# A two-layer cross-attention and mixture-of-experts kernel: order of the work in its first stage

## The reference

```
x = x + L0_xattn(ctx, layernorm(x))      # 4 heads of 64; keys and values from the context and from x itself
x = x + L0_ffn(layernorm(x))             # 8 experts, the best 2 per token, relu, 1024 wide
x = x + L1_xattn(layernorm(x), ctx)      # 16 heads of 16; keys and values from the context alone
x = x + L1_ffn(layernorm(x))             # 8 experts, the best 2 per token, gated, 512 wide
```

## Time and profile before

| | |
|---|---|
| median of 3 runs | 1573.96 us (1572.23 to 1576.97) |
| the profiled execution | 1573.92 us |
| its span | 1572.2 us |
| TensorE busy | 1430.4 us (91%) |
| DVE busy | 1036.2 us (66%) |
| ACT busy | 829.4 us (53%) |
| POOL busy | 685.5 us (44%) |

### The profile page before, as it was taken

One profiled execution on the slowest core, in us unless ns is written; L12 is line 12 of the kernel. 1 busy time (PEld: TensorE's weight loads), 2 busy tenths in 40 slices (PEclk: granted clock), 3 DMA queues, 4 the chain that ended last, 5 costly groups with the idle time before them and its releaser, 6 DMA issues. The chain is left out here.

```text
span 1572.2 us, 35956 instructions
## 1 busy us (share of the span) xinstructions
PE 1430.4 (91%) x12426; PEld 1048.7 (67%) x12426; DVE 1036.2 (66%) x1991; ACT 829.4 (53%) x1513; POOL 685.5 (44%) x525
## 2 busy tenths in 40 slices
PE   8799999999986699999999978999978499999996
PEld 2433333333355589989899966777758389999885
DVE  5678888888768645555555427888958755455443
ACT  2678888887743245556555524667744032222221
POOL 2522212211110254555545425777752246666554
PEclk6899999999975699999999996999995599999998
DMA  5332333232238365556577433000016274334553
GB/s 166 111 108 82 102 115 132 82 115 74 81 105 299 110 181 132 145 141 161 130 200 192 103 71 107 23 6 28 29 30 240 86 226 68 62 66 68 109 136 49
DMA packets 114589, 175.77 MB, mean 112 GB/s; under 512 B 18992, under 2 KB 76644, under 8 KB 114148
## 3 DMA queue, kind: packets, MB, share of 16 engines
q1 hardware_dynamic: 84375, 132.93, 25.6%
q0 software_dynamic: 27264, 37.82, 13.7%
q10 hardware_dynamic: 2791, 2.84, 0.6%
HBM read 106.34 MB, written 67.23 MB: 110 GB/s over the span
## 5 line engine op out<-in xcount | busy, mean ns | idle before, releaser
L1601 PE MATMUL e_ph<-e_zTt,weights_a 128*128 128x256 f16 x3072 | 350.4, 275 | 2.0 <-DVE e_zTt L1695 2.0
L1601 PEld LDWEIGHTS e_ph<-e_zTt,weights_a 128*128 x3072 | 302.6, 99 | 39.4 <-issue 2.5
L1655 ACT ACTIVATE e_h<-e_ph,e_b 128x256 f32<-128x256 f32 (+1 forms) x312 | 123.6, 453 | 185.9 <-PE e_ph L1601 185.6
L1551 POOL DMA_INDIRECT token_rows<-e_ysb,slot_token x71 | 128.4, 1808 | 172.2 <-DVE e_ysb L1734 158.0
L1615 PE MATMUL e_pyt<-weights_b,e_hh 128*128 x1136 | 192.7, 273 | 1.2 <-DVE e_ysb L1734 1.1
L1541 POOL DMA_INDIRECT gathered<-token_parts,slot_token x138 | 141.6, 1026 | 54.4 <-issue 46.7
L1717 DVE TENSOR_TENSOR e_hl<-e_h,e_hh 128x512 f16<-128x512 f32 x142 | 94.8, 690 | 103.5 <-ACT e_hh L1666 103.5
L680 PE MATMUL middle_banks<-probs,v 128*64 128x512 f32 (+1 forms) x576 | 152.9, 613 | 8.7 <-ACT raw_o L811 7.9
L1551 POOL DMA_INDIRECT out_dram<-e_ysb,slot_token x71 | 113.2, 1594 | 106.0 <-DVE e_ysb L1737 75.1
L935 DVE TENSOR_TENSOR acc<-acc,probs 128x1024 f32<-128x1024 f32 (+1 forms) x112 | 138.6, 1238 | 27.4 <-ACT probs L804 24.8
L1615 PE MATMUL e_pyt<-weights_b,e_hl 128*128 x568 | 154.8, 273 | 0.0
(11 more groups left out here) (274 smaller groups left out, 2805.6 us busy)
## 6 DMA issues: line engine op xcount, KB each, us to landing
weight_parts<-w_split SPq DMA_DIRECT2D x32, 512.0 KB, 3.4
weights_a<-weight_parts SPq DMA_DIRECT2D x16, 1024.0 KB, 7.4
x_sb<-weight_parts SPq DMA_DIRECT2D x14, 1024.0 KB, 6.9
x_sb<-in_u SPq DMA_DIRECT2D x24, 512.0 KB, 4.9
weight_parts<-x_sb SPq DMA_DIRECT2D x24, 512.0 KB, 3.4
w_raw<-in_w1T SPq DMA_DIRECT2D x16, 512.0 KB, 4.4
w_raw<-in_w2T SPq DMA_DIRECT2D x16, 512.0 KB, 4.8
weights_b<-weight_parts SPq DMA_DIRECT2D x8, 1024.0 KB, 9.5
```

Source lines behind the costliest of these rows:

```text
L1551: pool.indirect_dma_start(g.rows[layer], at, ysb[:, s, c, :], None, compute_op=ALU.add).then_inc(sto[s], 16)
L1601: last = pe.matmul(out[:, f, :], weights_up(i, e, wp, k, per[i] * q + f), zTs[:, s, 2 * zp + k, 0:cols[i] * P], start=(n == 0), stop=(n == 5))
L1655: last = act.activation(parted(hidden(h32, n), i)[:, f, :], parted(ph[:, bank_of(i, q)], i)[:, f, :], ACT.Relu, bias=b1[:, bass.ds(e, 1), ...
```

## The change

- ACT issues 11 loads instead of 14: gain and shift of the context norm come as one array put together on the host (`ln_x`), and those of the token norm likewise on SP (`ln_l`). Layer 2's value weights go ahead of its mask, its key weights and the small rows. Each group has a semaphore of its own.
- SP loads batch 0 of the tokens right behind the context, then the projection weights, batch 1, the small rows, batches 2 and 3. At the stage's end it waits only for the small rows.
- TensorE makes layer 2's values right behind the first turn (four idle products between), in the upper half of `kv`'s banks; then comes the turn of `zc`, layer 2's keys, and last the context's keys and values. Layer 2's mask is put on the turned context (DVE) and no longer on the keys, and ACT spreads the keys with a factor per partition that holds the scale.
- Row statistics, summary and root in this stage are those of batch 0 alone. Batch 1's are taken in the attention's head (two tiles in each of four steps), batches 2 and 3 in the slots of batch 0 (one tile a slot), with roots on POOL after tile 5 and after batch 1's roots.
- The context's keys leave the stage raw (`kraw`), with the sums of their squares (`ssc`). Root, norm, halves and the turning of the halves are done in the attention's head, the turning in the upper banks ahead of the first `turn_parts`.

The diff, cut to its core:

```
 # first stage, sync
-sp.wait_ge(ld_w, 32)
-for i in range(B): (load token rows of batch i)
+rows_in(0)
 (load wqkv, wo0)
+rows_in(1)
+sp.dma_start(g.glbl[:], a["ln_l"]).then_inc(ld_small, 16)
 (load bo)
+for i in range(2, B):
+    rows_in(i)
+sp.wait_ge(ld_small, 32)
-sp.wait_ge(ld_next, 16 * 5)
-for arrived in g.x_in:
-    sp.wait_ge(arrived, 16)
 # first stage, scalar: order behind the products
+act.wait_ge(v1_mm, 1)
+act.wait_ge(made, 3)
+own_v = kv[:, 2:4, :].rearrange("p b (h o d) -> p b h o d", o=2, d=HD1)
+for b in range(2):
+    for o in range(2):
+        act.copy(g.v1[:, 2 * b:2 * b + 2, o:H1:2, o * HD1:(o + 1) * HD1].rearrange("p b h d -> p (b h) d"),
+                 own_v[:, b, :, o, :]).then_inc(v1_ev, 1)
+act.wait_ge(k1_mm, 1)
+act.wait_ge(odd_known, 1)
+for hg in range(2):
+    for o in range(2):
+        act.activation(g.k1[:, :, hg, o, :], tr[:, hg, 0:B * M].rearrange("p (b m) -> p b m", b=B), ACT.Copy,
+                       scale=odd_head[:, o:o + 1]).then_inc(k1_ev, 1)
 act.wait_ge(ld_next, 16 * 2)
 (high halves of wqkv, wo)
 act.wait_ge(kv_done, 1)
 act.activation(sq[:], kv[:, :, 0:D], ACT.Square).then_inc(sq_done, 1)
+act.copy(g.kraw[:], kv[:, :, 0:D]).then_inc(sq_done, 1)
 act.copy(g.vctx[:], kv[:, :, D:2 * D]).then_inc(sq_done, 1)
 # first stage, tensor
 turn(ctx, 0)
-keep_going(14)
+keep_going(4)
+pe.wait_ge(ld_v1, 32)
+pe.wait_ge(ev, 2)
+(layer 2's values into kv[:, 2 + b // 2, ...])
 pe.wait_ge(v_step, 13)
 turn(zc, 2)
-keep_going(4)
+pe.wait_ge(ld_k1, 32)
+pe.wait_ge(mask_step, 5)
+(layer 2's keys from the masked context into tr[:, hg, ...])
 pe.wait_ge(ev, 4)
 pe.wait_ge(ld_w, 32)
 for b in range(B):
+    if b == 2:
+        pe.wait_ge(v1_ev, 4)
     (keys and values of the context)
-(layer 2's values and keys, turning of the key halves)
 # attention, tensor, scalar, gpsimd, vector
+        if t < 2:
+            pe.wait_ge(kt_ev, 2)                  # in turn_parts
-pipeline([(turn_z, 0, 2), (project, 1, 2), (turn_parts, 4, 0),
+pipeline([(turn_z, 0, 2), (project, 1, 2), (lambda l: l == 0 and turn_context(), CONTEXT_AT, 0), (turn_parts, 4, 0),
+context_high()                                    # scalar, behind gain_and_shift(1)
+          (lambda l: l == 0 and context_out(), CONTEXT_AT, 0), (parts_out, 4, 0),
+pool.tensor_tensor(rnc[:], g.ssc[:], g.neghalf[0:M, 0:B * H0], ALU.pow).then_inc(kr_done, 1)
+for t in range(TB // 2):
+    root(t, t % 2)
+pool.wait_ge(kt_ev, 2)
+        if t == TB - 3:
+            roots(pool, g, 2, TB, 2 * TB, g.first_steps, g.first_roots)
+    if b == 1:
+        roots(pool, g, 3, 2 * TB, T, g.first_steps, g.first_roots)
+    if t in (TB, 2 * TB):
+        dve.wait_ge(g.first_roots, t // TB + 1)   # in center
+context_norm()                                    # vector, behind ln_low(1)
+context_low()
+          (second_rows, 1, 0),
+        if b == 0:
+            later_rows(j)
+def second_rows(l):
+    if l >= TB // 2:
+        return
+    dve.wait_ge(g.x_in[1], 16)
+    for t in (TB + 2 * l, TB + 2 * l + 1):
+        dve.bn_stats(g.stats[:, t, :], g.x[:, t, :]).then_inc(x_step, 1)
+    if l == TB // 2 - 1:
+        dve.wait_ge(x_step, TB)
+        summarise(dve, g, 2, TB, 2 * TB, True, g.first_steps)
+def later_rows(j):
+    if j < 2 * TB:
+        t = 2 * TB + j
+        dve.wait_ge(g.x_in[t // TB], 16)
+        dve.bn_stats(g.stats[:, t, :], g.x[:, t, :]).then_inc(x_step, 1)
+    elif j == 2 * TB:
+        dve.wait_ge(x_step, 3 * TB)
+        summarise(dve, g, 3, 2 * TB, T, True, g.first_steps)
```

More of the change, by code:

```diff
@@ L123, in attention0_inputs @@
         lnT = m.sb("lnT_c", [P, 2, B, M])
-        gx = m.sb("gx", [P, 2])
-        bx = m.sb("bx", [P, 2])
+        gbx = m.sb("gbx", [P, 4])
+        gx, bx = gbx[:, 0:2], gbx[:, 2:4]
+        ctxT = m.sb("ctxT", [P, 2, 2, B, M])
+        wk1 = m.sb("wk1", [P, 2, D])
+        wv1 = m.sb("wv1", [P, 2, D])
+        own = m.sb("own", [P, 8])
+        own2 = m.sb("own2", [P, 8])
+        odd_head = m.sb("odd", [P, 2])
         wqkv = m.sb("wqkv", [P, 2, 3 * D])
@@ L307, in _ @@
-            dve.wait_ge(v_step, 20)
+            dve.wait_ge(ld_q, 16 * 3)
+            dve.scalar_tensor_tensor(g.gain[:], gq[:], SCALE0, gk[:], ALU.mult, ALU.mult).then_inc(g_step, 1)
+            dve.wait_ge(g_step, 1)
+            dve.tensor_reduce(gabs[:], g.gain[:], AX.X, ALU.max, apply_absolute_value=True).then_inc(g_step, 1)
+            dve.wait_ge(g_step, 2)
+            dve.tensor_scalar(g.shift[:, B:B + 1], gabs[:], -float(HD0), None, ALU.mult).then_inc(g_step, 1)
+            dve.tensor_scalar(g.shift[0:M, 0:B], mask[:], 1.0, -MASKED, ALU.subtract, ALU.mult).then_inc(g_step, 1)
@@ L398, in summarise, with roots @@
     dve.tensor_scalar(ve, tmp[:, 0, :], grow / D, eps, ALU.mult, ALU.add).then_inc(steps, 1)
[L401 to L404 removed]
+def roots(pool, g, run, t0, t1, steps, rooted):
+    pool.wait_ge(steps, 7 * run)
+    pool.tensor_tensor(g.rstd[:, t0:t1], g.stat_ve[:, t0:t1], g.neghalf[:, t0:t1], ALU.pow).then_inc(rooted, 1)
 def attention0(nc, g, a):
@@ L507, in attention0 @@
         LAG = 4
+        CONTEXT_AT = 3
         def pipeline(stages):
@@ L725, in between, with turn_context @@
                     project(tile)
+            def turn_context():
+                pe.wait_ge(kh_done, 1)
+                pe.wait_ge(kl_done, 1)
+                for n in range(2):
+                    for h in range(2 * B):
+                        last = pe.transpose(hi[:].bitcast(F16)[:, n, h * MP:h * MP + M],
+                                            khl[:, n, 2 * h:2 * h + 2, :].rearrange("p o d -> p (o d)"), g.ident16[0:M, 0:M])
+                last.then_inc(kt_done, 1)
             turn_z(0)
@@ L827, in output_high, with context_high, context_out @@
                 act.copy(o16[:, 0, u % 2], oT[:, u % 2]).then_inc(o_hi, 1)
+            def context_high():
+                act.wait_ge(kn_done, 1)
+                act.copy(khl[:, 0], kn[:]).then_inc(kh_done, 1)
+            def context_out():
+                act.wait_ge(kt_done, 1)
+                for n in range(2):
+                    act.copy(g.kctx[:, n, :, 0:M],
+                             hi[:].bitcast(F16)[:, n, 0:2 * B * MP].rearrange("p (h m) -> p h m", m=MP)[:, :, 0:M]
+                             ).then_inc(kt_ev, 1)
             gain_and_shift(0)
             gain_and_shift(1)
+            context_high()
             squares(0)
             squares(1)
-            pipeline([(gain_and_shift, 0, 2), (squares, 1, 2), (high, 3, 0), (parts_out, 4, 0),
+            pipeline([(gain_and_shift, 0, 2), (squares, 1, 2), (high, 3, 0),
+                      (lambda l: l == 0 and context_out(), CONTEXT_AT, 0), (parts_out, 4, 0),
                       (lambda l: l in pieces_head and weight_high(pieces_head[l]), 1, 0),
@@ L1134, in _ @@
         def _(pool):
-            roots(pool, g, 3 + 2 * layer, LAST, T)
+            roots(pool, g, 2 + 2 * layer, LAST, T, g.stat_steps, g.stat_roots)
             pool.iota(rev[:], pattern=[[-1, E]], base=E, channel_multiplier=0,
```

238 lines of the change are left out of this document (94 added, 144 removed).

## The result

The changed kernel takes 1575.81 us (median of 20 runs, 1572.64 to 1579.13) against 1571.70 for the kernel before on the same chip (20 runs, 1565.78 to 1576.97): ratio 1.0029, 95% interval 1.002 to 1.0038, so 3.1 to 6.0 us slower. I had forecast 15 us faster; the rival that was nearest is B, the low clock. The kernel before has two kinds of execution: of 80 taken beside the experiments, 41 have a mean granted clock of 0.922 or more and a median of 1567.8 us, and 39, like the profiled one (0.917), have 0.921 or less and a median of 1573.8 us, while 19 of the changed kernel's 20 lie at 0.913 to 0.919; the ratios here are to the mixture. The profiled execution of the changed kernel has a span of 1572.4 us.

A forecast was written before the change was run, and what follows sets the result against it. The first stage was taken to be bound by a TensorE chain of products at granted clock 0.50. 1573.92 - 19.2 (first stage) + 3.2 (head) + 0.8 (batch 0) = 1558.7 us; 8-in-10 range 1554.7 to 1578.

The forecast's parts named there:

- B: Rival, first stage: low clock returns, products take 30.4 us, attention starts at 41.9 (-4.3); 1573.6 us, no change; chance 0.46 to A, 0.38 to B.
- Start of the products: First stage: TensorE starts layer 2's value products at 7.9 us, behind ACT's 11 loads and two copies.
- the late end: First stage: products start at 10.1 us if the value weights' load again takes 7.6 us.
- the early end: First stage: products start at 7.9 us, with one megabyte of token rows around the weight loads instead of four.
- B's first reason: First stage: the clock is low because the products start late; the other reason was that its first rise fails.
- A: The forecast itself: high clock holds in the first stage, products take 15.4 us; 1558.7 us; chance 0.46.
- My argument against A from float32: First stage: the products are float32 throughout, which was held to speak against the high clock holding.
- Tail: First stage's end: ACT's squares and two copies, 3 x 1.02 = 3.1 us, plus 0.54 before the first `center`.
- Head: Attention's tiles 0 to 7: key work hidden, DVE's added statistics and summary on the path; +3.2 us, between 0 and 4.8.
- Batch 0: Attention's batch 0: 7.3 us more DVE work, mostly in idle time, and tile 16's `center` waiting for a root; +0.8 us.
- Rival C: Batch 0: DVE's added work ends up on the path, 7.3 us in place of 0.8; slower, 1580.1 us; chance 0.16.
- The sum: Whole kernel: first stage -19.2, head +3.2, batch 0 +0.8 against 1573.92 us, giving 1558.7 us.

The follow-up runs named there:

- e6_order_alone: The changed kernel with only ACT's loads reordered: value weights first, context's own weights behind layer 2's key weights; 1557.0 us, ratio 0.9903 to the kernel before.
- e10_sp_held: The changed kernel with SP waiting for the value weights before issuing batch 0's rows and all behind them; 1558.4 us, ratio 0.9942 to the kernel before.
- e8_all_rows: The changed kernel with all four batches' row statistics, summaries and roots in the first stage; 1572.3 us, ratio 1.0008 to the kernel before.
- e3_rows_back: The changed kernel with batch 1's row statistics, summary and root moved back into the first stage; 1571.7 us, ratio 1.0011 to the kernel before.

## Why the prediction was wrong, point by point

- **Start of the products: the step that failed.** ACT's side was right (last issue ends at 7.44, forecast 7.1; copies done at 8.2, forecast 7.9). I then took 7.9 for the start and kept 10.1, the old 7.6 us for the value weights, as the other end. They took 7.4 and 8.1, and TensorE was released at 11.21. So even the late end was too early: it went by the first of the two loads, and the trace before had the second at 8.5 us (shown with the result), which from 3.06 gives 11.6. My reason for the early end, one megabyte of rows now where four stood before, counted only batch 0 and left out the projection weights and batch 1, which SP issues before or beside them. `e6_order_alone`, with the value weights issued ahead of those loads, and `e10_sp_held`, with those loads held back, put the start at 8.72 and 8.38. The Trainium skill, "DMA: Bandwidth & Descriptors", section "Issuing engines are not separate DMA queues", which I quoted and outweighed, says that SP's and ACT's transfers interleave on the same engines; the trace agrees (8.1 us for 64 KB beside SP's loads, 3.8 without).
- **Clock.** Rival B's mechanism, for B's first reason, the late start. Its price was near: 30.4 us of products forecast, 30.2 measured; it came from 11.2 and not 7.9, which with a tail 0.4 shorter makes -1.6 of its -4.3. A's price was near too: 15.4 forecast, 16.3 in `e6_order_alone`, which lands at 1557.0 where A stood at 1558.7. My argument against A from float32 falls. The same products are busy 16.20 of 16.28 us at 1.00 in `e6_order_alone`. The Trainium skill, "TensorE: Matmul & The Clock Gate", section "Why this matters for your kernels", says that keeping TensorE continuously busy gets it to the high clock. The trace of the change disagrees again: busy 30.19 of 30.20 us at 0.50.
- **Tail.** 3 x 1.02 + 0.54 = 3.6 forecast; 41.4 to 44.6, 3.2, measured: right to 0.4.
- **Head.** +3.2 forecast, +4.26 measured. DVE's statistics are 2.8 of it (3.1 against `e8_all_rows`), within 2.5 to 3.55; the 1.5 of the second fall of the clock (1.1 against `e8_all_rows`) was not in the sum. That the key work would be hidden there is neither shown nor refuted.
- **Batch 0.** +0.8 forecast, +1.0 measured; without the statistics (`e8_all_rows`) +0.5. `center` of tile 16 waits for POOL, but DVE idles only 0.44 there. Rival C did not happen.
- **The sum.** -1.6 + 4.3 + 1.0 = +3.7 by the marks of the two profiles, 3.1 to 6.0 by the times. The two do not measure the same: the profile before is of the kind at the lower mean clock, the times are to both kinds.

## What to carry to other kernels

Where a chain of TensorE bounds a stage, read the granted clock and the last idle stretch ahead of it before its order: here that level was worth 13.5 us at the first `center` (44.60 against 31.14), the new order with the clock held 2.8 at tile 16's turn (174.04 against 176.82). For the first operand of a chain that is moved forward, add up all bytes that any queue has issued before it lands. Work taken out of a stage into a full engine's queue is paid there, so part each mark of the path and look at all parts. Before a median is used as a yardstick, list the mean granted clock of every execution behind it: here the kernel before had two kinds, 6 us apart, and one profile shows only one of them.

## What the runs showed of the hardware that was not expected

- The same float32 products ran at 0.50 for 30.2 us in the change and at 1.00 for 16.3 us in `e6_order_alone`, busy nearly without a break in both (30.19 of 30.20 us, 16.20 of 16.28). In `e10_sp_held` they began at 0.53 us each and went on at 0.30, so the clock can rise while they run. What decides is not shown.
- The granted clock reads 1.00 from the start of these profiles, though six warm-up matmuls at 2.51 take 0.46 us each, and 0.23 each later; in `e10_sp_held` it reads 1.00 from 8.38 to 10.40 beside products of 0.53 us. Ahead of the first fall that a profile's rows show, go by the length of the matmuls.
- The length of one idle stretch does not tell alone whether the clock falls: 1.72 us ahead of tile 6's turn kept it in the kernel before and in `e8_all_rows` and lost it in `e3_rows_back`.
- A transfer of 64 KB took 8.1 us beside 3 MB of another queue's (the change), 3.8 us with those held back (`e10_sp_held`).
